# Local attention: POOL scales the probabilities by the inverse row sums, in halves; half of the reciprocal root runs ahead of the masks

## The reference, cut to what matters

```python
q, k, v = split(shift_token(x) @ wqkv)        # 8 heads of 64
q = l2norm(q) * qs ; k = l2norm(k) * ksc
q, k = rotary_xpos(q, k)
# windows of 128 tokens; each sees itself and the window before
sim = einsum('bhwid,bhwjd->bhwij', 8 * q, look_around(k))
attn = softmax(where(mask, -max, sim))
out = einsum('bhwij,bhwjd->bhwid', attn, look_around(v))
x = x + out @ wo
```

## Time and profile before

| | us |
|---|---|
| median of three runs | 2179.41 (2178.56 to 2180.12) |
| the profiled execution | 2177.43 |
| its span in the trace | 2175.6 |
| PE / PE weight loads busy | 1994.9 / 1708.5 |
| DVE / ACT / POOL busy | 1556.9 / 1090.1 / 414.4 |

### The profile page before, as it was taken

One profiled execution on the slowest core, in us unless ns is written; L12 is line 12 of the kernel. 1 busy time (PEld: TensorE's weight loads), 2 busy tenths in 40 slices (PEclk: granted clock), 3 DMA queues, 4 the chain that ended last, 5 costly groups with the idle time before them and its releaser, 6 DMA issues. The chain is left out here.

```text
span 2175.6 us, 43248 instructions
## 1 busy us (share of the span) xinstructions
PE 1994.9 (92%) x13920; PEld 1708.5 (79%) x13920; DVE 1556.9 (72%) x4621; ACT 1090.1 (50%) x2533; POOL 414.4 (19%) x257
## 2 busy tenths in 40 slices
PE   6799999999999967999999969995999999968998
PEld 6678878878878856888888758884888888857887
DVE  5536636645645657999999757775889999957777
ACT  3332222222323226888888734442777777753343
POOL 0100000000000003444444300001444444420010
PEclk9899999999999989999999989998999999988999
DMA  7100000000000020000000010002000000000002
GB/s 257 49 1 1 1 2 1 1 2 1 1 2 1 1 103 2 6 6 5 5 5 5 5 61 11 10 10 64 5 5 5 5 5 6 5 15 15 11 10 82
DMA packets 43266, 42.77 MB, mean 20 GB/s; under 512 B 8514, under 2 KB 37913, under 8 KB 43164
## 3 DMA queue, kind: packets, MB, share of 16 engines
q1 hardware_dynamic: 41030, 36.17, 5.2%
q10 hardware_dynamic: 2134, 5.26, 0.6%
HBM read 33.02 MB, written 8.39 MB: 19 GB/s over the span
## 5 line engine op out<-in xcount | busy, mean ns | idle before, releaser
L887 ACT ACTIVATE l_probs<-l_probs,l_negmax 128x256 f32<-128x256 f32 x512 | 253.1, 496 | 64.9 <-DVE l_negmax L968 64.9
L115 PE MATMUL ps<-local_w_hi,l_xT 128*128 128x512 f32 x384 | 167.1, 435 | 37.1 <-DVE l_xT L961 31.1
L841 POOL TENSOR_TENSOR l_t<-l_t,l_t 128x1024 f32<-128x1024 f32 x64 | 152.9, 2389 | 195.3 <-DVE l_t L1014 195.3
L392 ACT ACTIVATE attn_exp<-ps 128x512 f32<-128x512 f32 x130 | 77.7, 598 | 205.9 <-PE ps L117 205.9
L115 PE MATMUL ps<-attn_w_hi,attn_xT_hi 128*128 128x512 f32 x392 | 168.8, 431 | 12.7 <-issue 10.1
L845 POOL TENSOR_TENSOR l_t<-l_t,l_rnorm 128x1024 f32<-128x1024 f32 x64 | 121.9, 1905 | 307.3 <-DVE l_rnorm L985 307.3
L893 ACT ACTIVATE l_probsT<-ps 128x512 f32<-128x512 f32 x256 | 138.3, 594 | 50.4 <-PE ps L1112 50.4
L116 PE MATMUL ps<-attn_w_lo,attn_xT_hi 128*128 128x512 f32 x392 | 158.5, 404 | 0.0
L117 PE MATMUL ps<-attn_w_hi,attn_xT_lo 128*128 128x512 f32 x392 | 158.1, 403 | 0.0
L117 PE MATMUL ps<-local_w_hi,l_xT 128*128 128x512 f32 x384 | 155.0, 404 | 0.0
L116 PE MATMUL ps<-local_w_lo,l_xT 128*128 128x512 f32 x384 | 154.6, 403 | 0.0
(11 more groups left out here) (212 smaller groups left out, 5859.1 us busy)
## 6 DMA issues: line engine op xcount, KB each, us to landing
tok_x<-x SPq DMA_DIRECT2D x16, 512.0 KB, 4.2
m_shifted<-shifted SPq DMA_DIRECT2D x20, 256.0 KB, 2.8
shifted<-x SPq DMA_DIRECT2D x64, 64.0 KB, 1.5
out<-x SPq DMA_DIRECT2D x8, 512.0 KB, 4.4
ffn_w_raw<-ffn_w SPq DMA_DIRECT2D x6, 640.0 KB
local_w_raw<-ffn_wqkv SPq DMA_DIRECT2D x4, 768.0 KB, 5.3
h<-txt SPq DMA_DIRECT2D x4, 512.0 KB, 4.6
attn_w_raw<-attn_Wq ACTq DMA_DIRECT2D x1, 1024.0 KB, 6.4
```

Source lines behind the costliest of these rows:

```text
L115: nc.tensor.matmul(out, wh, mh, start=start, stop=False, skip_group_check=True)
L392: nc.scalar.activation(ex[:, at % 2], ps[:, at % 2], ACT.Exp).then_inc(s.attn_exp.sem, 1)
L841: nc.gpsimd.tensor_tensor(t1[:], t1[:], t2[:], ALU.add).then_inc(s.summed.sem, 1)
L887: last = nc.scalar.activation(v, v, ACT.Exp, bias=nb[:, h:h + 1], scale=-1.0, accum_out=rsum[:, h:h + 1])
```

## The change

- POOL no longer spreads the inverse sums. It multiplies the exponentials themselves by them, in place, one instruction of 128x512 for each pair of heads (`normalise`). The reciprocals come in two halves of four heads (`inverse`): the first at the end of the step with the masks, the second at the start of the next.
- The transposes `inverses`, the copy L924 and the product L1047 go. ACT rounds the attention output and DVE takes its rest straight from PSUM.
- PE makes the output product ahead of pairs 0 and 1, and the value product between pairs 1 and 2. Pairs wait for POOL's product instead of for the exponentials.
- POOL makes the even mask (128x128) instead of DVE.
- `rnorm(0)` is a `tensor_reduce` (the larger of the sum and a stored floor). `rnorm(0)` to `rnorm(4)` run before `x_lo`; the other six run in twos behind masks 1, 2 and 3. The edge column of the next x (L961) comes behind mask 0.

```diff
-            def spread_out(t):
...
-            def window(t, late=True):
...
+            def normalise(t, r):
+                for pair in range(LPAIRS):
+                    if pair % 2 == 0:
+                        pool.wait_ge(*s.inverted.after(2 * t + pair // 2 + 1))
+                    v = pm[:, pair].rearrange("p (e k) -> p e k", e=2)
+                    nc.gpsimd.tensor_tensor(v, v, rinv[:, 2 * pair:2 * pair + 2].unsqueeze(2).to_broadcast([P, 2, 2 * P]),
+                                            ALU.mult).then_inc(s.scaled.sem, 1)
+            def even_mask(t):
+                wait(pool, s.masked, 4 * (t - 1))
+                nc.gpsimd.tensor_tensor(mask_e[:, P:2 * P], prev[:], negs[:, bass.ds(t // 2, 1)].to_broadcast([P, P]),
+                                        ALU.add).then_inc(s.mask_set.sem, 1)
+            def window(t, r):
+                if r == 1:
+                    even_mask(t - 1)
...
             with pool.Fori(2, T // 2) as p:
-                window(2 * p)
+                window(2 * p, 0)
+                normalise(2 * p - 1, 1)
...
-                window(2 * p + 1)
+                window(2 * p + 1, 1)
+                normalise(2 * p, 0)
...
-                    nc.scalar.activation(oth[:], on[:], ACT.Copy).then_inc(s.o_hi.sem, 1)
+                    wait(act, s.o_full, n - 2)
+                    nc.scalar.activation(oth[:], ps[:, OT], ACT.Copy).then_inc(s.o_hi.sem, 1)
...
-                    return nc.vector.tensor_scalar(ss[:], ss[:], 1e-24, None, ALU.max)
+                    return nc.vector.tensor_reduce(ssc[:], ss[:], AX.X, ALU.max)
...
+            def inverse(t, half):
+                heads = slice(4 * half, 4 * half + 4)
+                wait(dve, s.exped, 4 * t + 2 * half + 2)
+                wait(dve, s.scaled, 4 * (t - 1) + 2 * half + 2)
+                nc.vector.reciprocal(rinv[:, heads], rsum[:, heads]).then_inc(s.inverted.sem, 1)
...
-                    nc.vector.tensor_tensor(otl[:], on[:], f32(oth[:]), ALU.subtract).then_inc(s.o_done.sem, 1)
+                    nc.vector.tensor_tensor(otl[:], ps[:, OT], f32(oth[:]), ALU.subtract).then_inc(s.o_done.sem, 1)
...
+                if a:
+                    root(5)
                     x_lo(n + 1, 1 - r)
                 for h in range(LH):
                     if b:
...
                         score(n - 1, h, mask)
-                    if a:
-                        chain.wait()
-                        if 3 + h < LAST:
-                            chain.mark(rnorm(3 + h))
-                        else:
-                            rnorm(LAST).then_inc(s.rnorm.sem, 1)
-                if c:
-                    wait(dve, s.o_full, n - 1)
-                    wait(dve, s.r_out, n - 1)
-                    nc.vector.tensor_tensor(on[:], ps[:, OT], on[:], ALU.mult).then_inc(s.o_norm.sem, 1)
+                    if a and h == 0:
+                        x_edge(n + 1, 1 - r)
+                    if a and h:
+                        root(2)
+                if b:
+                    inverse(n - 1, 0)
...
             def probs_t(t, pair):
-                wait(pe, s.exped, 4 * t + pair + 1)
+                wait(pe, s.scaled, 4 * t + pair + 1)
```

More of the change, by code:

```diff
@@ L752, in local_phase @@
     HF = DH // 2
-    (idle, one, xc, xt, sq, t1, t2, qt, kt, vv, pm, pt, on, spread, oth, otl, cos, sin, mask_e, mask_o, prev, flags, negs, qks,
-     ss, rn, tmp, nb, rsum, rinv, mean, rs, nmr, tmp32, dev), _ = mem.place(
+    (idle, xc, xt, sq, t1, t2, qt, kt, vv, pm, pt, oth, otl, cos, sin, mask_e, mask_o, prev, flags, negs, qks,
+     ss, ssc, rn, tmp, nb, rsum, rinv, mean, rs, nmr, tmp32, dev), _ = mem.place(
         K.mlp_end, mem.end,
-        (f"l{layer}_idle", [P, 1], F32), (f"l{layer}_one", [P, 1], F32), (f"l{layer}_x", [P, 2, D], F32),
+        (f"l{layer}_idle", [P, 1], F32), (f"l{layer}_x", [P, 2, D], F32),
         (f"l{layer}_xT", [P, 2, 2, 2 * XW], F32R), (f"l{layer}_sq", [P, 2, LINNER], F32),
@@ L822, in _ @@
             nc.gpsimd.memset(K.w_raw[:, KC * W1C + HC * D:FW], 0.0).then_inc(s.padded.sem, 1)
-            nc.gpsimd.memset(one[:], 1.0)
+            nc.gpsimd.memset(ss[:], 1e-24)
             nc.gpsimd.memset(kt[:, 1], 0.0)
@@ L846, in window @@
                                         ALU.mult).then_inc(s.rotated.sem, 1)
+            pool.wait_ge(*s.const_in.after(160))
             for t in range(4):
[L849 removed]
+                window(t, t % 2)
+                if t:
+                    normalise(t - 1, 1 - t % 2)
             with pool.Fori(2, T // 2) as p:
[L851 removed]
+                window(2 * p, 0)
+                normalise(2 * p - 1, 1)
                 pool.wait_ge(*s.ffn_hi.after(p - 1))
@@ L882, in exps @@
                 if pair == 0:
-                    wait(act, s.inverted, t)
+                    wait(act, s.inverted, 2 * t)
                 for e in range(2):
@@ L1022, in step, with root @@
                 if a:
-                    nc.vector.tensor_reduce(ss[:], sq[:].rearrange("p a (h d) -> p (a h) d", d=DH), AX.X,
+                    nc.vector.tensor_reduce(ss[:, :, 0], sq[:].rearrange("p a (h d) -> p (a h) d", d=DH), AX.X,
                                             ALU.add).then_inc(s.sq_summed.sem, 1)
[L1025 to L1029, removed]
+                k = 0
+                def root(ops):
+                    nonlocal k
+                    for _ in range(ops):
+                        if k > LAST:
+                            return
+                        if k == 0:
+                            wait(dve, s.sq_summed, n + 1)
+                        else:
+                            chain.wait()
+                        if k == 1:
+                            wait(dve, s.rotated, n)
+                        if k < LAST:
+                            chain.mark(rnorm(k))
+                        else:
+                            rnorm(LAST).then_inc(s.rnorm.sem, 1)
+                        k += 1
+                if a:
+                    root(5)
                     x_lo(n + 1, 1 - r)
@@ L1032, in step @@
                     if b:
+                        if h == 0 and r == 1:
+                            wait(dve, s.mask_set, (n + 1) // 2)
                         if h % 4 == 0:
@@ L1126, in values @@
                 last.then_inc(s.o_full.sem, 1)
-            def inverses():
-                for pair in range(LPAIRS):
-                    last = nc.tensor.transpose(ps[:, RB, pair * P:(pair + 1) * P],
-                                               spread[:, pair * P:(pair + 1) * P],
-                                               K.ident[:])
-                last.then_inc(s.r_t.sem, 1)
             def step(n, r, a, b, c, d):
@@ L1163, in step @@
                 if c:
+                    probs_t(n - 2, 0)
+                    wait(pe, s.p_done, 4 * (n - 2))
+                    probs_t(n - 2, 1)
+                if b:
+                    wait(pe, s.v_done, n - 1)
+                    project(1 - r, 2, V).then_inc(s.v_full.sem, 1)
+                if c:
                     for pair in (2, 3):
@@ L1173, in step @@
                     x_t(n + 1, 1 - r)
-                if c:
-                    wait(pe, s.spread, n - 1)
-                    wait(pe, s.p_done, 4 * (n - 1))
-                    inverses()
                 if b:
@@ L1185, in step @@
                     wait(pe, s.v_done, n - 1)
+                    wait(pe, s.p_done, 4 * (n - 1))
                     wait(pe, s.y_done, n - 2)
@@ L1539, in __init__ @@
         self.p_done = count("p_done")
-        self.r_t = count("r_t")
-        self.r_out = count("r_out")
-        self.spread = count("spread")
         self.inverted = count("inverted")
+        self.scaled = count("scaled")
+        self.mask_set = count("mask_set")
         self.sq_summed = count("sq_summed")
```

45 lines of the change are left out of this document (10 added, 35 removed).

## The result

The changed kernel takes 2199.34 us (median of four runs, 2198.73 to 2200.89) against 2179.76 for the kernel before, run beside it: a ratio of 1.0092, 95% interval 1.0074 to 1.0109. It is 20 us slower. The forecast was 2190, in a range of 2166 to 2207. The direction is right and the forecast change, +11, is about half of the measured one. What is missing lies in two terms: the steady steps cost 19.8 us where 15 were forecast, and everything outside them gained nothing where a gain of 4 was forecast (19.6 by the medians, less 19.8, is -0.2; the interval of the ratio leaves -3.7 to +4.0). The profiled executions, 2200.89 and 2177.43, lie on the far sides of their medians, so their spans differ by 23.5.

The account below looks back on a forecast made before the run. PE nearly bounds the kernel, but a ring through root, POOL's product and PE's transposes sets the 13.23 us step, with a second close behind. 2177.4 + 15 - 4 = 2188.4, as a median 2190; range 2166 to 2207.

Parts of the forecast that it names:

- The second ring: Masks, exponentials, ACT's rounding, cosine product, POOL's sum, next mask: 13.09 us before, 13.50 after, setting the step.
- M to E: First mask (M) to ACT's rounding of the attention output (E): 5.16 us a step, 4.85 before.
- E to M: ACT's rounding to the next first mask: 8.16 us through DVE and POOL, 8.09 through PE.
- The seed held: DVE's `rnorm(1)`, taken to be held until POOL's sum ends, some 0.7 to 0.8 us long instead of 0.18.
- PE's way: ACT's rounding through PE's output product, pairs, `x_t` and scores to the next mask: 8.09 us.
- PE's gap ahead of x_t: PE waits for the copy of pair 2: pairs 2 and 3 take 1.33 us, idle 0.4 to 0.5.
- POOL's products at 1.0: POOL's four 128x512 products of exponentials and inverses take 1.0 us each, bounds 0.93 and 1.20, costing nothing.
- Rival 3: POOL too late: at 1.2 us a product its sum slips every second step, +14 on the forecast, 2204; chance 0.13.
- rival 4: DVE's masks and POOL exclude each other, 1.9 us a step, +106, 2296; chance 0.05 together with unknown.
- Rivals 1, 2 and 5: PE's order bounds, 2162, chance 0.19; root not held, 2182, and scaling costs what it saves, 2176, together 0.17.
- Fill and drain -4: First steps taken at 0, drain of each layer at -2 us (-0.5 to -3), -4 in all.
- +15: Steady steps: 0.27 us longer each, over 28 steps and two layers.

Follow-up runs that it names:

- h1: Changed kernel with PE's old order, POOL's sum cut to the query half (keys lack their sine part, measuring only): 2152.59 us, ratio 0.9871.
- e2: Changed kernel with PE's order of before (pairs 0 and 1, output product, pairs 2 and 3, value product): 2192.35 us, ratio 1.0051.
- e1: Changed kernel with the six late root instructions one behind each of masks 1 to 6 instead of in twos: 2192.91 us, ratio 1.0053.
- e5: Changed kernel with the old root arrangement: three ahead, edge column ahead of the masks, one behind each mask: 2199.88 us, ratio 1.0085.
- f2: Changed kernel with PE's old order, roots 0,1,1,2,1,1,0,0 behind masks, even mask in POOL's other step, ACT's squares before value copy: 2165.43 us.
- k2: f2 with PE's order of the change instead of the old one: 2180.55 us, ratio 1.0001.
- k1: Kernel before the change with one edit, ACT's squares ahead of its copy of the values: 2181.32 us, ratio 1.0007.
- f1: Changed kernel with PE's old order, roots 0,1,1,2,1,1,0,0 behind the eight masks, even mask in POOL's other step: 2177.01 us, ratio 0.9988.

## Why the prediction was right, and where it was off

- **The second ring decides.** Right. Shown by h1 (0.60 off the hold is 0.60 off the step) and e2 (PE's slack, same step). The step came to 13.58 for 13.50.
- **M to E 5.16.** Measured 5.30 after odd and 5.37 after even masks, where the edge column takes 0.22 for 0.17; this is the mis-sized term of the step. The prices of 0.20 and 0.34 held up to mask 3 (M + 1.70, forecast 1.71). From mask 3 to mask 4, with two roots and the memset between, it is 0.80 where I had 0.68 (0.34 + 0.20 + 0.14), so mask 5 comes at M + 2.85 for 2.73 and pair 2's exponentials, which wait for it, at 3.31 for 3.18. From there on the distances are as forecast. The trace of the kernel before had this price, and the sum did not use it: there the same two masks, with one root and the memset between, start 0.61 apart, and a second root's 0.20 gives 0.81.

```profile
1021.62 0.42 DVE L968 CUSTOM_DVE_ANT_0 l_probs<-ps,l_mask_even 128x256 f32<-128x256 f32 x1
...
1022.23 0.42 DVE L968 CUSTOM_DVE_ANT_0 l_probs<-ps,l_mask_even 128x256 f32<-128x256 f32 x1
```

- **E to M 8.16.** Measured 8.06 and 8.11. This was 0.08 too long where M to E was 0.17 too short, so part of the miss in the step was hidden by luck. The seed held, as taken: 0.77, over within 0.05 of POOL's sum in both steps. The output product came at E + 1.35 for 1.48, so PE's way did not get ahead.
- **PE's gap ahead of x_t.** Pairs 2 and 3 to `x_t` are 1.36 for 1.33. PE's idle time is 0.33 ahead of `x_t` (0.4 to 0.5 forecast) and 0.59 ahead of the output product in every second step (0.1 to 0.5 forecast). Its waits in 900 to 1200 us, with the output product's and POOL's (total us, times, longest):

```profile
POOL l_t L848 <- DVE l_t L1025: 26.1, 22, 1.9
...
PEld ps L115 <- DVE l_oT_lo L1012: 12.4, 22, 0.8
PEld ps L1112 <- issue: 12.3, 22, 0.6
```

  The root product no longer holds PE's loads, as forecast; where the earlier trace rows had 13.3 us, these two waits of 12.4 and 12.3 stand now.
- **POOL's products at 1.0.** 4.04 for four, 64.9 of 100 us busy; right. Rival 3 (POOL late) stayed out by 0.43 and appeared in e1 and e5, as soon as the exponentials were on time. I had it decide from 1.1 a product; it decides as well from an earlier E, a condition the rival did not name.
- **Masks beside POOL.** 0.42, not held; rival 4 is out. Rivals 1, 2 and 5 are out by the step: 13.58, with E to M above 7.8 and M to E above 5.16.
- **Fill and drain -4.** Not borne out. By the medians all that lies outside the steady steps came to -0.2, by the two traces to +3.7, of which +1.9 are in the fills and drains of the local attention. The fills, taken at 0, were 1.6 and 0.8 longer. The drains, taken at -2 each, were +1.1 and -1.6. The -1.6 was measured at nearly one clock, so there the forecast was close; the +1.1 was measured at 0.83 for 0.94, and the sum had no term for the clock. PE's new order has a part in it too: 1.4 to 2.0 us a drain, by e2 against the changed kernel and f2 against k2. That pairs stand there behind an output product that is late, or is not there to cover them, would explain this and is not shown.

In sum +15 became +19.8, and -4 became -0.2: +20 by the medians for the forecast +11. The mechanism of the step was right; its term M to E was 0.17 too small, and the ends were priced without the clock.

The Trainium skill (SBUF — State Buffer, the section "Who interferes with whom") says that a DVE instruction with at most one SBUF input, outside the two-port modes, does not contend with POOL, while `tensor_scalar` can enter such a mode. Masks, which read PSUM and one SBUF operand (0.42 both ways), and a seed of sixteen columns (0.17 free, 0.77 to 2.02 beside POOL's sum) agree with it, the smallest of instructions included. In which mode the seed ran no view shows.

## What to carry to other kernels

Before a ring of waits is shortened, measure every other ring that is within some tenths of it: here a ring that was worked out at 13.09 stood behind a step of 13.23, and the change paid into the hidden one. An instruction that is held until another engine's instruction ends is worth nothing to move ahead unless it gets past the end of that one; it only pulls what follows it ahead of the work that was waiting. And an engine that is 65% busy can still be the late one: read the idle time ahead of the one instruction that the ring needs (0.43 here, 0 in e1) rather than the busy share, and put its other work in the step that has room (0.40 moved, 0.35 a long step gained). Last, read the granted clock beside every time taken in the first and last steps of a loop: the same drain took 25.63 at 1.00 and 27.76 at 0.88.

## What the runs showed of the hardware

- The seed, a `tensor_scalar` of 128x16 in int32, takes 0.17 alone (h1) and was held to 0.77 (changed kernel), 1.10 (f2), 1.61 (e1) and 2.02 (e5), each time to within 0.05 of the end of POOL's 128x1024 sum. A reciprocal of 128x4 and small `tensor_reduce` beside POOL kept 0.17 to 0.19.
- POOL: 128x512 with one operand spread takes 1.01 (4.04 for four); 128x1024 the same way 1.9; the sum of two full streams 2.37 for 1024 columns and 1.30 for 512.
- The steady stretch (900 to 1000 us) ran at a granted clock of 1.00 in both kernels. The drains ran at means from 0.80 (k1) to 1.00, and in f1 and h1 a drain at 1.00 was 2.1 and 2.4 us shorter than the same kernel's drain at 0.88. What decides the clock there is open.
- Not tried: whether the root's instructions with two SBUF inputs (L993, L994) would be held by POOL's sum if the seed were not there. In all kernels but h1 the seed had waited the sum out, and in h1 the sum was already over.
